# The retrieval layer of a decoder: three of four token tiles take gathered table rows, the fourth keeps the dense products

## The chip, the cores and the metric

The kernel runs on one core of one Trainium2 chip. The metric is the device time of one execution in microseconds. The whole decoder of twelve layers is one program; the change concerns the last layer alone.

## The reference

The layer is a memory of 4096 experts, each one row of a down table and one row of an up table, found by product keys, beside a small gated MLP. For each of 4096 tokens (B 4, T 1024, D 256):

```python
q = (x @ w_queries.T).reshape(b, t, 2, 4, 32)               # 2 sides, 4 heads
sim = einsum('btphn,hkpn->pbthk', q, keys)                  # 128 keys a side and head
sx, ix = top_k(sim[0], 8); sy, iy = top_k(sim[1], 8)
all_scores = (sx[..., :, None] + sy[..., None, :])          # 64 pairs a head
all_idx = ix[..., :, None] * 128 + iy[..., None, :]
scores, pos = top_k(all_scores, 8)
indices = take_along_axis(all_idx, pos)                     # above 4095: the last row is read
ew = silu(einsum('btd,bthkd->bthk', x, down_embed[indices])) * softmax(scores)
experts = einsum('bthk,bthkd->btd', ew, up_embed[indices])
mlp = silu(x @ w_gate.T) * (x @ w_up.T) @ w_down.T          # inner width 512
x = layernorm(x + mlp + experts)
```

A token has 4 heads x 8 picks = 32 picks.

## The kernel before

The residual stays in SBUF, transposed: `chip.xt` is [128, 2, 4096], features on the partitions in two chunks. The layer works on 32 tiles of 128 tokens. It gathers nothing. For each tile TensorE multiplies the tokens with all 4096 rows of the down table ("dots", 8 chunks of 8 matmuls, L3811), ScalarE takes silu of each chunk into `r_active` [128 rows, 32 blocks, 128 tokens], and VectorE multiplies this by a dense matrix of weights ("mix", L3981), nonzero where a token picked the row. TensorE then multiplies the result with all rows of the up table ("out", 8 chunks of 8 matmuls, L3851), adding to the MLP's result in PSUM.

The dense weights are made from one-hots. VectorE finds the keys (MAX8 and FIND_INDEX8, "keys", L3993 and L3991) and the best pairs ("pairs", L4010 and L4008). POOL decodes the position of a pair into the two key numbers ("decode", L3914 to L3943) and compares the second number with 0..127, one lane at a time (`r_second_hot`, L3950, 32 instructions a tile). VectorE makes the one-hot of the first number times the softmax weight (`r_first_hot`, L4034 and L4035). For each lane two small matmuls (L3824) put their product into PSUM: four batches of 16 matmuls a tile.

The order is written out by hand. `retrieval_slots` makes one list of steps for all engines: in slot s, tile s has its weights made and multiplied, tile s+1 its dots, tile s-1 its out product, tile s+2 its keys and pairs, tile s+3 its query projection ("project") and similarities ("sims"). A slot has 8 places, each with one chunk of dots and one of out. "gate" and "hide" are the MLP, "add" adds the residual into `norm_sum`, and "mean", "var", "spread" are the layer norm of a group of four finished tiles. Every engine walks the same list and does its part of each step; semaphores order them. The products of "project", "sims", "gate", "mean", "var" and "spread" go through a ring of two PSUM banks, each used in turn; dots, weights and outputs have two banks each. SyncE issues seven loads at the start, down table third, up table last.

`step(...)` (L51) opens a block with its own semaphores; `load`, `Chip` and the other layers are not touched. The line number of a semaphore wait at the end of a block is L56 or L64.

Of the kernel before, what the change touches and what calls it, by code (L numbers as in the profile page):

```python
# [5 lines left out]
F32 = mybir.dt.float32  # L6
# [7 lines left out]
P = 128  # L14
# [3678 lines left out]
LANES = SLOT // 2  # L3693
CHUNKS = 8
BATCHES = 4


def retrieval_slots():

    order = []  # L3700
    for s in range(-3, TOKEN_TILES + 2):
        closes = (s - 5) // PER_HALF if s >= 5 and s % PER_HALF == 1 else None
        places = [[] for _ in range(CHUNKS)]
        places[0] += [("add", s - 2, 0), ("exp", s + 1, 0), ("lanes", s, 1), ("decode", s + 1, 0)]
        places[1] += [("gate", s, 0), ("weights", s + 1, 0)]
        places[3] += [("hide", s, 0)]
        places[4] += [("project", s + 3, 0), ("turn", s + 1, 0), ("lanes", s + 1, 0)]
        places[6] += [("sims", s + 3, 0)]
        for n in range(RHEADS * SIDES):
            places[1 + n // 3].append(("keys", s + 2, n))  # L3710
        for n in range(RHEADS):
            places[5 + n // 2].append(("pairs", s + 2, n))
        places[7].append(("shift", s + 2, 0))
        for j in range(CHUNKS):
            here = [("mix", s, j // 2)] if j % 2 == 0 else []
            here += [("out", s - 1, j), ("dots", s + 1, j)] + places[j]
            order += [step_ for step_ in here if 0 <= step_[1] < TOKEN_TILES]
            if closes is not None:
                order += [(kind, closes, 0) for kind, at in (("mean", 1), ("var", 3), ("spread", 6)) if at == j]
    return order  # L3720


def retrieval_ffn(chip):
# [3 lines left out]
    order = retrieval_slots()  # L3727
    ring = {}
    for kind, t, n in order:
        for use in {"gate": ("gate", "up"), "sims": ("sims_0", "sims_1"), "project": ("project",), "mean": ("mean",), "var": ("var",), "spread": ("spread",)}.get(kind, ()):  # L3730
            ring[(use, t)] = len(ring)
    with ExitStack() as ctx:
# [4 lines left out]
        active = sb("r_active", [P, 2, BLOCKS, P])  # L3737
        second_hot, first_hot = sb("r_second_hot", [P, 2, LANES, KEYS]), sb("r_first_hot", [P, 2, LANES, 2 * BLOCKS])
# [17 lines left out]
        with step(nc, "search_loaded down_loaded mlp_loaded up_loaded ring_ready bank_read_0 bank_read_1 dots_ready dots_active weights_ready mixed hot_first hot_second "  # L3756
# [5 lines left out]
            def read_of(use, t):  # L3762
                r = ring[(use, t)]
                return bank_read[r % 2], r // 2 + 1
# [483 lines left out]
```

## Time and profile before

| | before |
|---|---|
| median of 3 runs | 10450.3 us (10445.38 to 10500.5) |
| profiled execution: its time | 10466.0 us |
| profiled execution: span | 10464.2 us |
| TensorE busy | 8774.6 us (84%) |
| VectorE busy | 5572.0 us (53%) |
| ScalarE busy | 4189.2 us (40%) |
| POOL busy | 2222.1 us (21%) |
| TensorE's mean granted clock | 0.892 of full |

PE is the matmul side of TensorE and PEld its weight loads; DVE is VectorE, ACT ScalarE, POOL GpSimd, SP SyncE. Names of tiles are printed without digits, L12 is line 12 of the kernel. The shares are means over the whole program; the layer that is changed fills the last 1500 us of it, and its rows are taken from there.

### The profile page before, as it was taken

The numbers are of one execution on the slowest core, as the hardware profiler recorded it, in microseconds if no ns is written. First come the engines' busy times: TensorE is split into PE (matmuls) and PEld (weight loads), VectorE is DVE, ScalarE is ACT, GpSimd is POOL, SyncE is SP. The second block draws the span as 40 slices with busy tenths as digits, with TensorE's granted clock in tenths as the row PEclk, the third lists the DMA queues.
The fourth block names the chain that finished last, engine by engine and source line by source line (L and its number), as shares of the span: only waits on it lengthen the run. The fifth ranks groups of instructions, "written<-read, shape, count | busy, mean of one in ns | idle before, by whom it ended". The sixth has DMA issues, their size and how long they took to land. (4 is left out here: it accounts for less than half of the span.)

```text
span 10464.2 us, 134852 instructions
## 1 busy us (share of the span) xinstructions
PE 8774.6 (84%) x51394; PEld 5200.4 (50%) x51506; DVE 5572.0 (53%) x9096; ACT 4189.2 (40%) x6715; POOL 2222.1 (21%) x2590
## 2 busy tenths in 40 slices
PE   4888583985898979999996988889886999999999
PEld 1222242652333346646643544444343444799998
DVE  6777441014776736526634887765544666343343
ACT  3666230111555546415622676652221444222221
POOL 1010112011111001101100443330000110566665
PEclk8888675985999989999997998989886999999999
DMA  3222142111222100000000000000001322100000
GB/s 67 41 41 41 36 66 78 65 57 39 41 41 41 24 22 1 4 13 7 1 4 14 1 1 1 1 3 8 6 1 29 58 45 44 44 1 1 1 1 17
DMA packets 161954, 263.21 MB, mean 25 GB/s; under 512 B 38699, under 2 KB 78485, under 8 KB 159543
## 3 DMA queue, kind: packets, MB, share of 16 engines
q1 hardware_dynamic: 155175, 240.91, 11.4%
q0 software_dynamic: 6144, 13.64, 0.4%
q8 instruction: 421, 6.90, 0.3%
q14 instruction: 214, 1.75, 0.1%
HBM read 165.30 MB, written 75.53 MB: 23 GB/s over the span
## 5 line engine op out<-in xcount | busy, mean ns | idle before, releaser
L819 ACT ACTIVATE probs<-scores 128x1024 f32<-128x1024 f32 (+4 forms) x960 | 868.4, 937 | 873.6 <-PE scores L696 618.4
L908 DVE TENSOR_REDUCE row_max<-ring 128x1 f32<-128x512 f32 (+3 forms) x1792 | 1025.4, 628 | 238.5 <-PE ring L670 213.5
L696 PE MATMUL scores<-query_stack,key_stack 99*128 99x512 bf16 (+3 forms) x2816 | 846.2, 391 | 164.4 <-DVE levels L930 77.8
L716 PE MATMUL outputs<-probs,head_values 128*32 128x512 f32 (+3 forms) x5632 | 778.5, 627 | 101.3 <-ACT probs L816 98.6
L3950 POOL TENSOR_SCALAR r_second_hot<-constants,r_picks_t 128x128 f32<-128x128 f32 x1024 | 662.2, 664 | 431.2 <-DVE r_picks_t L4027 431.2
L816 ACT ACTIVATE probs<-levels,quant 128x1024 f32<-128x1024 uint8 x512 | 612.7, 1233 | 330.3 <-DVE levels L930 327.0
L930 DVE TENSOR_SCALAR levels<-scores 128x1024 uint8<-128x1024 f32 x512 | 607.7, 1220 | 181.4 <-PE scores L696 149.3
L670 PE MATMUL ring<-key_stack,query_stack 96*128 96x512 bf16 (+3 forms) x1792 | 607.9, 382 | 62.5 <-DMA key_stack<-normed_parts 39.9
L696 PEld LDWEIGHTS scores<-query_stack,key_stack 99*128 99x128 bf16 x2816 | 256.6, 103 | 684.6 <-DVE levels L930 278.6
L3676 DVE TENSOR_TENSOR_SCAN ssm_pre<-ssm_pre,added 128x1024 f32<-128x1024 f32 x256 | 571.0, 2271 | 33.2 <-ACT ssm_pre L3634 33.2
L3891 ACT ACTIVATE r_active<-r_psum_dots 128x512 f32<-128x512 f32 x256 | 152.7, 597 | 999.4 <-PE r_psum_dots L3811 995.3
L3981 DVE TENSOR_TENSOR r_active<-r_psum_weights,r_active 128x1024 f32<-128x1024 f32 x128 | 156.8, 1225 | 713.5 <-PE r_psum_weights L3824 713.5
L3611 PE MATMUL state_sums<-term,constants 128*128 128x512 f32 x1024 | 493.4, 605 | 43.9 <-POOL term L3642 34.3
L3851 PE MATMUL r_psum_y<-r_active,r_up_rows 128*128 128x128 f32 x4096 | 511.0, 279 | 0.0
L3811 PE MATMUL r_psum_dots<-residual,r_down_rows 128*128 128x128 f32 x4096 | 502.5, 276 | 3.0 <-DMA r_down_rows<-in_L_ffn_down 2.5
L3029 POOL TENSOR_TENSOR norm_squares<-qk,rope 128x256 f32<-128x256 f32 x256 | 181.3, 743 | 1517.4 <-DVE qk L2953 1517.4
L3851 PEld LDWEIGHTS r_psum_y<-r_active,r_up_rows 128*128 128x128 f32 x4096 | 479.1, 192 | 18.9 <-issue 10.5
L3811 PEld LDWEIGHTS r_psum_dots<-residual,r_down_rows 128*128 128x128 f32 x4096 | 481.4, 193 | 5.2 <-DMA r_down_rows<-in_L_ffn_down 3.3
L670 PEld LDWEIGHTS ring<-key_stack,query_stack 96*128 96x128 bf16 x1792 | 171.0, 103 | 497.3 <-DVE row_max L908 298.4
L2760 PE MATMUL window_products<-wide_w,shifted 128*128 128x512 f32 x768 | 366.8, 629 | 53.8 <-DVE shifted L2930 45.2
L3648 POOL TENSOR_TENSOR added_rows<-ssm_du_rows,ssm_state_in_rows 128x384 f32<-128x384 f32 x256 | 208.3, 832 | 927.0 <-SPq L56 906.5
L3630 ACT ACTIVATE added_rows<-ssm_du_rows,ssm_state_in_rows 128x128 f32<-128x128 f32 x1280 | 398.1, 386 | 4.3 <-PEq L64 4.3
(657 smaller groups left out, 16553.3 us busy)
## 6 DMA issues: line engine op xcount, KB each, us to landing
joined_heads<-heads_out SPq DMA_DIRECT2D x512, 32.0 KB, 2.0
expert_w<-in_L_ffn_w SPq DMA_DIRECT2D x16, 1024.0 KB, 11.5
quant_parts<-parts SPq DMA_DIRECT2D x48, 256.0 KB, 5.2
query_stack<-quant_parts SPq DMA_DIRECT2D x48, 256.0 KB, 8.6
key_stack<-quant_parts SPq DMA_DIRECT2D x48, 256.0 KB, 8.4
query_stack<-cross_parts SPq DMA_DIRECT2D x48, 256.0 KB, 8.2
normed_parts<-parts SPq DMA_DIRECT2D x48, 256.0 KB, 4.8
query_stack<-normed_parts SPq DMA_DIRECT2D x48, 256.0 KB, 8.6
```

Of the source, the lines that this page charges most:

```text
L670: last = nc.tensor.matmul(out[:, 0:cols], lhs, k_stack[0:max_row, h, j * GROUP:j * GROUP + cols], start=True, stop=not edge)
L696: last = nc.tensor.matmul(out[:, off:GROUP], keys, q_stack[0:rows, h, half * GROUP + off:(half + 1) * GROUP], start=True, stop=not edge)
L716: last = nc.tensor.matmul(o_ps[SLOT * i:SLOT * (i + 1), half % out_banks, off:GROUP], vals, probs[0:k_rows, n % 2, i // 2, i % 2, off:GROU ...
L816: nc.scalar.activation(dst, levels[:, e % 2, :, :], ACT.Exp, bias=quant[:, 4:5], scale=scale).then_inc(probs_ready, 1)
L819: nc.scalar.activation(dst, s_ps[0:k_rows, 2 * (e % 2):2 * (e % 2) + 2, off:GROUP], ACT.Exp, scale=scale).then_inc(probs_ready, 1)
L908: nc.vector.reduce_max(row_max[:, i, qt, at:at + 1], src[:, 0:cols], AX.X).then_inc(ring_read, 1)
L930: ts(levels[:, e % 2, :, :], s_ps[:, 2 * (e % 2):2 * (e % 2) + 2, :], 0.0, QMAX, ALU.max, ALU.min).then_inc(scores_read, 1)
L3611: last = nc.tensor.matmul(sum_ps[:, half(j)], chip.c(C_ID), term[:, i % 2, half(j)], start=(n == 0), stop=(n == STATES - 1))
L3676: nc.vector.tensor_tensor_scan(state[:, i % 2, :], decay[:, i % 2, :], added[:, i % 2, :], 0.0, ALU.mult, ALU.add).then_inc(state_ready, 1)
L3811: last = nc.tensor.matmul(s_ps[:, k % 2, i * P:(i + 1) * P], down[:, c, row * P:(row + 1) * P], x(t, c), start=(c == 0), stop=(c == FC - 1))
L3851: last = nc.tensor.matmul(y_ps[:, t % 2, c * P:(c + 1) * P], up[:, row, c * P:(c + 1) * P], active[:, t % 2, row, :], start=False, stop=(r ...
L3950: last = ts(second_hot[:, n, q, :], chip.c(C_IOTA), picks_t[:, t % 2, 1, lane:lane + 1], None, ALU.is_equal)
```

## The change

Of each group of four tiles, the first three are now *fetched* and the fourth is *dense*.

For a fetched tile POOL issues 32 indirect DMAs (768 in all), one a pick: each brings for all 128 tokens their row of a new input `L3_ffn_tables` (down and up row side by side, 512 floats, 2 KB; padded to 16384 rows so that every index is valid) into one slot of the ring `r_got` of 16 slots. VectorE takes the dot product of the down half with the token's own features (`rows`, transposed back by TensorE and copied by ScalarE) with a tensor_tensor_reduce. After the eight dots of a head ScalarE takes silu ("live"), VectorE multiplies by the softmax share ("weigh"), ScalarE makes for each pick a diagonal matrix (identity times the 128 weights), and TensorE multiplies the up half of the slot with it, adding in PSUM ("mix", two matmuls a pick). POOL waits before every fourth gather until the four picks that used the slots are summed.

The dense tile goes the old way, with single instead of double buffers (`r_active`, the dots bank), batches of 8 lanes, and the second one-hot made by one VectorE instruction for 8 lanes. POOL's decoding moves to VectorE ("places", "codes", "picked"), shorter by a few instructions. POOL does nothing but gathers.

The new list `retrieval_events` runs in beats of eight rows. Fetched tile i has the beats 4i to 4i+3 (one head each); a group is 12 beats, all are 96. A beat has 8 places, one dot in each; the mixing of the head before stands in places 1 to 4. A tile's search is spread over five beats, three beats ahead of its gathers; the dense tile's dots take beats 1 to 8 of its group, its weights beats 8 to 13, its out product beats 13 to 20. The layer norm of a group now covers the dense tile of the group before and its own three fetched tiles, so there are 9 closings instead of 8. The load of the down table moves behind the three of the MLP.

The diff, cut to its core:

```diff
+GOT_ROWS = 16
+RELEASE = 4
+CYCLE = FETCHED * RHEADS
+def retrieval_events():
...
+    for g in range(GROUPS):
+        for r in range(PER_HALF):
+            t = PER_HALF * g + r
+            s = CYCLE * g + FETCHED * (r - 2)
+            put(s - 2, 5, "project", t)
+            put(s - 2, 7, "queries", t)
+            put(s - 1, 3, "sims", t)
+            put(s - 1, 5, "sims_copy", t)
+            for n in range(RHEADS * SIDES):
+                put(s + n // 4, 2 * (n % 4) + 1, "keys", t, n)
+            for n in range(RHEADS):
+                put(s + 2, 2 * n, "pairs", t, n)
+            put(s + 2, 7, "shift", t)
+            put(s + 3, 0, "places", t)
+            put(s + 3, 2, "exp", t)
+            put(s + 3, 3, "codes", t)
+            put(s + 3, 6, "picked", t)
+            put(s + 4, 3, "weights", t)
+        for r in range(FETCHED):
+            i = FETCHED * g + r
+            first = RHEADS * i
+            put(first - 3, 5, "gate", i, r)
+            put(first - 3, 6, "gated", i, r)
+            put(first - 2, 0, "multiplied", i, r)
+            put(first - 1, 5, "hide", i, r)
+            put(first - 2, 5, "rows", i)
+            put(first - 2, 7, "rows_copy", i)
+            put(first + RHEADS + 1, 2, "add", i, r)
         for j in range(CHUNKS):
+            put(CYCLE * g + 1 + j, 6, "dots", g, j)
+            put(CYCLE * g + 1 + j, 7, "silu", g, j)
+            put(CYCLE * (g + 1) + 1 + j, 5, "out", g, j)
+        put(CYCLE * g + 7, 4, "turn", g)
+        for n in range(BATCHES):
+            put(CYCLE * g + 8 + n, 7, "lanes", g, n)
+            put(CYCLE * g + 9 + n, 5, "weave", g, n)
+            put(CYCLE * g + 10 + n, 3, "blend", g, n)
...
+    for i in range(FETCHED_TILES):
+        for h in range(RHEADS):
+            k = RHEADS * i + h
+            for n in range(TOP):
+                plan.setdefault((k, n), []).insert(0, ("dot", k, n))
+            plan.setdefault((k + 1, 0), []).append(("live", k))
+            plan.setdefault((k + 1, 1), []).insert(0, ("weigh", k))
+            for n in range(TOP):
+                put(k + 1, 1 + n // 2, "mix", k, n)
...
+            @block.gpsimd
+            def _(pool):
+                for i in range(FETCHED_TILES):
+                    pool.wait_ge(decoded, searched[fetched_tile(i)] + 1)
+                    for n in range(PICKS):
+                        k = PICKS * i + n
+                        if k >= GOT_ROWS and n % RELEASE == 0:
+                            pool.wait_ge(summed, k - GOT_ROWS + RELEASE)
+                        nc.gpsimd.indirect_dma_start(out=got[:, k % GOT_ROWS, :], out_offset=None, in_=io["L3_ffn_tables"],
+                                                     in_offset=bass.IndirectOffsetOnAxis(ap=index[:, i % FETCHED, n:n + 1], axis=0)).then_inc(arrived[k % GOT_ROWS], 16)
...
+                    elif kind == "mix":                       # TensorE
+                        k, n = which
+                        i = k // RHEADS
+                        pe.wait_ge(diagonal_ready, TOP * k + n + 1)
+                        for c in range(FC):
+                            last = nc.tensor.matmul(y_of(i, 0)[:, c * P:(c + 1) * P], got[:, (TOP * k + n) % GOT_ROWS, DIM + c * P:DIM + (c + 1) * P], diagonal[:, n, :],
...
+                    elif kind == "live":                      # ScalarE
+                        k = which[0]
+                        act.wait_ge(dot_ready, TOP * (k + 1))
+                        nc.scalar.activation(act_w[:, k % 2, :], dot[:, k % 2, :], ACT.Silu).then_inc(live_ready, 1)
+                    elif kind == "mix":
+                        k, n = which
+                        if n == 0:
+                            act.wait_ge(weighted, k + 1)
+                        if k:
+                            act.wait_ge(summed, TOP * (k - 1) + n + 1)
+                        nc.scalar.activation(diagonal[:, n, :], chip.c(C_ID), ACT.Copy, scale=act_w[:, k % 2, n:n + 1]).then_inc(diagonal_ready, 1)
...
+                    if kind == "dot":                         # VectorE
+                        k, n = which
+                        at, i = TOP * k + n, k // RHEADS
...
+                        if n == 0 and k >= 2:
+                            dve.wait_ge(diagonal_ready, TOP * (k - 1))
+                        dve.wait_ge(arrived[at % GOT_ROWS], 16 * (at // GOT_ROWS + 1))
...
+                        nc.vector.tensor_tensor_reduce(scratch[:, at % 2, :], got[:, at % GOT_ROWS, 0:DIM], rows[:, i % 2, :], 1.0, 0.0, ALU.mult, ALU.add,
+                                                       dot[:, k % 2, n:n + 1]).then_inc(dot_ready, 1)
+                    elif kind == "weigh":
+                        k = which[0]
+                        dve.wait_ge(live_ready, k + 1)
```

## Rows read from the trace of the kernel before

**Rows 1.** Windows: a stretch of the retrieval step, busy us of each engine.

```profile
core 0: us, PE busy (x) PEld busy (x) DVE busy (x) ACT busy (x) POOL busy (x), PEclk, DMA share, GB/s
9000.00:10400.00 1400.00, 1399.15 (x13698) 1339.78 (x13697) 544.98 (x1594) 322.77 (x488) 931.21 (x1506) 1.00 0.01 1
```

**Rows 2.** Chain of waits: start us, us, engine, line; counts include the weight loads.

```profile
9014.91 1.72 PE r_psum_ring L3801 x4
...
9026.82 1.79 PE r_psum_dots L3811 x16
9028.60 3.57 PE r_psum_ring L3833 x32
9032.18 1.93 PE r_psum_weights L3824 x32
```

**Rows 3.** Chain of waits: first and last pieces of the step.

```profile
8948.16 0.42 SPq L3772
...
10441.68 1.97 PE r_psum_ring L3859 x4
...
10445.77 1.93 PE r_psum_ring L3866 x16
...
10448.35 1.45 PE r_psum_ring L3872 x8
...
10449.82 0.69 DVE residual L4050
```

**Rows 4.** Instructions of one line: durations in ns, min/median/max.

```profile
L3950 POOL TENSOR_SCALAR r_second_hot<-constants,r_picks_t x1024: 590/596/1679, 8974.5 to 10405.1; 128x128 f32<-128x128 f32 x171
...
L4035 DVE TENSOR_TENSOR r_first_hot<-r_first_hot,r_picks_t x64: 1224/1274/2209, 8975.7 to 10403.4; 128x1024 f32<-128x1024 f32 x64
```

**Rows 5.** Timeline of POOL, expert layer: start us, us, instruction, idle before.

```profile
2303.02 0.94 POOL L2563 DMA_INDIRECT got<-produced,place_now  x1 [0.30 <-issue]
...
2315.51 0.94 POOL L2563 DMA_INDIRECT got<-produced,place_now  x1 [0.30 <-issue]
```

**Rows 6.** DMA, 2296 to 2330: GB/s in 40 slices; packets, MB, share.

```profile
GB/s 0 0 53 101 120 87 101 111 96 101 111 145 53 130 116 63 140 140 29 130 149 58 87 183 48 116 0 0 0 0 0 0 0 0 0 0 0 0 10 0
...
q0 software_dynamic: 768, 2.10, 23.3%
```

**Rows 7.** Timeline of VectorE: the first tile's search.

```profile
8959.39 0.28 DVE L3991 FIND_INDEX8 r_best_at<-r_best,norm_squares 128x8 uint32<-128x128 f32 x1
...
8959.85 0.28 DVE L3991 FIND_INDEX8 r_best_at<-r_best,norm_squares 128x8 uint32<-128x128 f32 x1
...
8962.57 0.41 DVE L4003 TENSOR_TENSOR r_sums<-r_best 128x256 f32<-128x256 f32 x1
...
8964.33 0.17 DVE L4016 TENSOR_TENSOR r_weight<-r_score 128x32 f32<-128x32 f32 x1
```

**Rows 8.** Timeline of VectorE in the expert layer.

```profile
2320.75 0.48 DVE L2576 SCALAR_TENSOR_TENSOR mixed<-got,gate_now,mixed 128x256 f32<-128x256 f32 x1
2321.15 0.35 DVE L2575 TENSOR_SCALAR mixed<-got,gate_now 128x256 f32<-128x256 f32 x1
```

**Rows 9.** The page's costliest groups: busy us, mean ns of one, idle before.

```profile
L3676 DVE TENSOR_TENSOR_SCAN ssm_pre<-ssm_pre,added 128x1024 f32<-128x1024 f32 x256 | 571.0, 2271 | 33.2 <-ACT ssm_pre L3634 33.2
```

**Rows 10.** Timeline of ScalarE: scaled copies in another layer, a table load here.

```profile
5902.90 1.55 ACT L3630 ACTIVATE added_rows<-ssm_du_rows,ssm_state_in_rows 128x128 f32<-128x128 f32 x5
5904.35 1.14 ACT L3634 ACTIVATE ssm_pre<-ssm_dt,a_log 128x1024 f32<-128x1024 f32 x1
...
8963.79 1.28 ACT L3891 ACT_TABLE_LOAD   x1
```

**Rows 11.** Windows of three other layers, columns as in rows 1.

```profile
200.00:400.00 200.00, 160.65 (x827) 50.61 (x820) 155.31 (x166) 132.38 (x119) 20.51 (x14) 0.89 0.18 34
...
5800.00:6000.00 200.00, 186.04 (x765) 102.57 (x764) 172.41 (x98) 144.11 (x332) 113.03 (x85) 0.99 0.00 1
8400.00:8600.00 200.00, 181.85 (x1363) 93.10 (x1363) 116.87 (x255) 92.88 (x124) 25.89 (x18) 0.92 0.34 55
```

**Rows 12.** Instructions of one line: the gathers of the expert layer.

```profile
L2563 POOL DMA_INDIRECT got<-produced,place_now x64: 942/946/1011, 2296.7 to 2419.9; - x64
```

More of the change, by code:

```diff
@@ L3692 @@
 TURN = P // SLOT
-LANES = SLOT // 2
+LANES = 8
 CHUNKS = 8
[L3695 to L3713, printed above, removed]
-        for j in range(CHUNKS):
[L3715 to L3720, printed above, removed]
@@ L3726, in retrieval_ffn @@
     rc = RINNER // P
-    order = retrieval_slots()
+    events = retrieval_events()
+    uses = {"gate": ("gate", "up"), "sims": ("sims_0", "sims_1"), "project": ("project",), "rows": ("rows",), "mean": ("mean",), "var": ("var",), "spread": ("spread",)}
     ring = {}
-    for kind, t, n in order:
-        for use in {"gate": ("gate", "up"), "sims": ("sims_0", "sims_1"), "project": ("project",), "mean": ("mean",), "var": ("var",), "spread": ("spread",)}.get(kind, ()):
-            ring[(use, t)] = len(ring)
+    for kind, *which in events:
+        for use in uses.get(kind, ()):
+            ring[(use, *which)] = len(ring)
+    searched = {t: n for n, t in enumerate(which[0] for kind, *which in events if kind == "picked")}
+    adds = {tuple(which): n + 1 for n, which in enumerate(which for kind, *which in events if kind == "add")}
     with ExitStack() as ctx:
@@ L3810, in _ @@
+                        for i in range(PER_CHUNK):
+                            row = PER_CHUNK * j + i
                             for c in range(FC):
-                                last = nc.tensor.matmul(s_ps[:, k % 2, i * P:(i + 1) * P], down[:, c, row * P:(row + 1) * P], x(t, c), start=(c == 0), stop=(c == FC - 1))
+                                last = nc.tensor.matmul(s_ps[:, i * P:(i + 1) * P], down[:, c, row * P:(row + 1) * P], x(PER_HALF * g + FETCHED, c), start=(c == 0), stop=(c == FC - 1))
@@ L3821, in _ @@
                             for r in range(2):
[L3822 removed]
+                                half = slice(P // 2 * r, P // 2 * (r + 1))
                                 out = w_ps[:, r, :].rearrange("p (s q i) -> p q s i", s=2, i=BLOCKS)[:, q, :, :]
[L3824 removed]
+                                last = nc.tensor.matmul(out, second_hot[half, q, :], first_hot[half, q, :], start=True, stop=True)
@@ L3854, in _ @@
                             last.then_inc(y_ready, 1)
                     elif kind == "mean":
-                        out = free_bank("mean", t)
-                        pe.wait_ge(added, PER_HALF * (t + 1))
+                        cols = closing(which[0])[0]
+                        out = free_bank("mean", *which)
+                        for n, r in ([(which[0] - 1, FETCHED)] if which[0] else []) + ([(FETCHED * which[0] + FETCHED - 1, FETCHED - 1)] if which[0] < GROUPS else []):
+                            pe.wait_ge(added, adds[(n, r)])
@@ L3864, in _ @@
-                        for p in range(PER_HALF):
+                        out = free_bank("var", *which)
+                        pe.wait_ge(c_squared, FC * (which[0] + 1))
+                        for p in closing(which[0])[2]:
                             for c in range(FC):
```

418 lines of the change are left out of this document (245 added, 173 removed).

## The prediction

> **What bounds the kernel now.** I read the page first, to see that only the last layer, the retrieval step, is touched, and then the windows of that step. In the 1400 us from 9000 to 10400 TensorE is busy in 1399.15 and its granted clock is 1.00; VectorE is busy in 545, ScalarE in 323, POOL in 931, the DMA engines in 1% [rows 1]. The step is bound by TensorE alone. The chain of waits says the same: it runs from one matmul group to the next, with no other engine between [rows 2]. A tile costs two dense products over all 4096 rows (16 chunks of 8 matmuls, 1.79 us a chunk), four groups of 16 small matmuls that make the weights (1.93 us each), gate and up (3.57), down (8 matmuls, as a chunk, 1.79), sims (1.72), the projection (four matmuls of the same 0.223 us, 0.9) and its share of a normalisation, 1.3. These are 45 to 46 us, and 32 tiles of it fill the step. The step begins with SyncE's first load at 8948.2 and its last VectorE piece ends at 10450.5 [rows 3]: 1502 us. Before and behind it nothing changes.
>
> **The unit of the new order.** It runs in beats: one head of one fetched tile, eight picks, is a beat, 3 tiles x 4 heads = 12 beats make a group of four tiles, 8 groups make 96 beats. So the new step is lead-in + 96 x T + tail, and the whole question is T. Four resources each have a floor for T.
>
> **TensorE.** Removed, in three tiles of four: both dense products (28.6 us) and the weights (7.7). Added there: 32 picks x 2 matmuls (64 x 0.223 = 14.3 us) and two transposes (0.45). Per group: mixing 42.9, dense dots and out of one tile 28.6, its weights 7.7, gate and up 14.3, down 7.2, projection 3.8, sims 6.9, transposes 1.3, closing matmuls 5.4 (1.97 + 1.93 + 1.45 [rows 3]). The sum is 118 us, or 9.84 us a beat, where four tiles cost 181 before. All this is at full clock.
>
> **POOL.** Its decoding and its 1024 one-hots (596 ns each [rows 4]) go; it only issues gathers, 768 of them. The layer with the experts has the same instruction: eleven of them start from 2303.02 to 2315.51, one in 1.25 us, 0.95 busy and 0.30 between [rows 5]. A row there is 1 KB per partition, here 2 KB, but the number of rows is 128 in both, so I keep 1.25: 10.0 us a beat, 960 in all. If the busy part went by bytes it would be 2 x 0.95 + 0.30 = 2.2 us (17.6 a beat); no row speaks for that, since the index list is what the instruction works through, and it stands as the far bound, with the price of rival (C).
>
> **DMA engines.** 16 to 17 of those gathers (2.10 MB) took 23.3% of 16 engines in 34 us [rows 6], 0.48 us for each. A new one moves twice the bytes: 0.48 us if the price goes by rows, 0.96 by bytes, so 3.8 to 7.7 us a beat. They are not the bound. The last gather is issued by 2316.5 and traffic ends in the slice that ends at 2318.1 (slices of 0.85 us [rows 6]), so a row lands some 1.6 us after its issue, 2.6 after its start.
>
> **VectorE.** Neighbouring instructions overlap, so I count start to start. Kept per tile: eight key searches at 0.46, pairs and shift from 8962.57 to 8964.50, three short ones of 0.2: 6.3 us [rows 7]. Taken over from POOL per tile: about eight short ones at 0.2 and three of 128x512 at 0.7 (0.69 [rows 3]): 3.7 us. Added: 96 dots of 128x256 with a sum. No row has this instruction. The plain two-input form of that shape lasts 0.41, or 0.33 start to start by the overlap seen [rows 7]; the scalar form lasts 0.48 and its successor starts 0.40 behind it [rows 8]; the scan's 2.2 ns an element would make 0.57 [rows 9]. I take 0.40, as nearest in kind, bounds 0.33 and 0.57. Per group: search 25, decoding 15, dots 38 (32 to 55), one-hots 10.4 (1.2 + 0.7 + 0.7, four times), blends 4.8, the rest (multiply, add, centre, scale, weigh) 10. That is 103 us, 8.6 a beat (8.1 to 10.0). ScalarE adds 96 scaled copies of 128x128; five of these run from 5902.90 to 5904.35, 0.29 each [rows 10]: 28 a group. With silus, copies and ten table loads of 1.28 [rows 10] it is near 61, 5.1 a beat. It is no bound, but a table load in front of a copy delays TensorE by 1.3 us.
>
> **How they meet.** Three floors, 10.0, 9.84 and 8.6, lie almost on one another, and each beat's work differs. TensorE's beats go from 7 us (weights and mixing) to 13.6 (mixing, two chunks, gate and up, projection, mean), VectorE's from 5.7 to 12.3 (decoding beside one-hots). The largest of the three in each of the 12 beats, added up, is 134 us, T = 11.1; perfect smoothing gives 10.0. The coupling allows only a part of it. A beat's dots are followed by silu, weighing, scaled copies and matmuls one beat later. While VectorE waits for the silu, the next dots and searches are queued behind it; while TensorE waits for the scaled copies, its chunks and the gate are, and for these VectorE's multiply waits a beat later. POOL reissues four slots when their four rows are summed. A row is held for 2.6 us plus some 1.35 beats, of the two beats that 16 slots last; at T = 11 the slack is 4.6 us, less than the overrun of some beats put together, and POOL, itself at its floor, can't catch up. TensorE, which now waits, also loses clock. Stages in which several engines take turns show what is left of it: busy share times granted clock is 0.71, 0.92 and 0.84 [rows 11]. With 9.84 us of work a beat these give T = 13.9, 10.7 and 11.7. I take the middle one, T = 11.7.
>
> **Lead-in and tail.** The key searches begin near 8959, the first shift is done at 8964.5 [rows 7]; decoding adds 3.7, the next tile's searches between some 1.8, the first gather 2.6: beat 0 starts near 8972.5, 24 us after the step began. On SyncE's queue the load of the down table moves behind those of the MLP; its reader comes a beat later, and that hides it. Behind beat 95: mixing 3.6, dense out 8 x 1.79, add 0.4, and a closing of one tile, about 5 where four tiles take 8.8 [rows 3]: 24 us. Together 48.
>
> **Sum.** 48 + 96 x 11.7 = 1171, against 1502: 331 less. The profiled execution took 10466.0 with a span of 10464.2; the median of the three is 10450.3, 16 below. Median predicted: 10450 - 331 = 10120.
>
> **The rivals.** (A) Smooth: POOL's pace alone, T = 10.0 to 10.8. At 10.0 the step is 1008, the time 9956. For it: the other floors are lower. Against: the uneven beats and the small slack. (B) The coupling costs more: a ring of two beats that starves POOL whenever TensorE overruns, table loads in the path, a clock that falls with the waits. T = 13 to 14.6; at 13.9 the step is 1382 and the time 10330. The share of 0.71 speaks for it, the two others against. (C) Slower, by one mechanism: a gather's issue is stretched while VectorE works from SBUF. Break-even is T = 15.15, a gather every 1.89 us. VectorE's instructions with two SBUF inputs (dots, comparisons, one-hots) would fill about 57 of 120 us; were the 0.95 us stretched to double by that, a gather would take 2.2, T = 17.6, step 1738, time 10686. For it: beside POOL's work, VectorE's 128x1024 multiply goes from 1224 to a median of 1274 and at most 2209 ns, and a POOL one-hot from 590 to at most 1679 [rows 4]. Against: the medians are 4% and 1% over the minima, not double, and 64 gathers lie within 942 to 1011 ns [rows 12], though hardly one of them ran beside such an instruction.
>
> The Trainium skill (SBUF — State Buffer, "Who interferes with whom") says that a two-input VectorE instruction takes only the read side of what it shares with GpSimd, that writing descriptors needs the write side, and that copies and tensor-scalars in a two-port mode are what block a GpSimd DMA. By that rule only the short decoding copies would hold gathers up, an estimated 6 us of a group, and T would grow by at most 0.5; no row here shows it.
>
> **How the numbers follow.** Forecast, T = 10.8 to 13.0 (10033 to 10244): 0.53. (A): 0.12. (B): 0.20. T near break-even, within 0.5%: 0.05. (C) and what else is slower: 0.10. A change within 0.5%, 52 us, is about what a measurement of this kernel can't tell from none. Faster is 0.85, same 0.05, slower 0.10. The range takes in the case of POOL's pace almost to its floor (T = 10.2, 9975) and (B) up to T = 13.9 (10330); VectorE's upper bound for the dots (10.0 a beat) lies inside.
>
> **What would show it.** Right: gathers start 1.25 us apart at the least; TensorE is busy in 85 to 90% of the step at a clock of 0.90 to 0.97; waits for dots are put down to gathers or ring slots; the step lasts 1130 to 1300 us. Wrong: a DMA_INDIRECT clearly over 1 us (C); a clock near 0.8 and long waits of TensorE for scaled copies (B); dots over 0.6 us, which makes VectorE the bound.

## The result and the profile after

The changed kernel takes 10667.4 us (median of 4 runs, 10659.2 to 10676.5) against 10464.9 for the kernel before, measured beside it: ratio 1.0186, 95% interval 1.0167 to 1.0206. The forecast was 10120, with a range of 9975 to 10330 and 0.85 for faster. It is slower, outside the range. By the formula of the prediction, T = (time - 8996) / 96, a beat lasts 17.4 us instead of 11.7. This T is the time in another unit, and so are those of the runs below (the expectations use values lower by 0.2). In the trace, from the first dot (8972.99) to the mixes of the last beat (10610.10), a beat lasts 17.05 us.

The windows of the retrieval step (its bounds, then busy time of each engine, granted clock, share of the DMA engines, GB/s) answer to [rows 1]:

```profile
9000.00:10600.00 1600.00, 1128.71 (x7832) 1044.68 (x7832) 732.08 (x3334) 457.93 (x1170) 733.55 (x744) 0.81 0.42 123
```

No engine is the bound now: TensorE is busy in 71% of the step and at a clock of 0.81, POOL in 46%, VectorE in 46%. The groups of that stretch (busy, mean ns | idle before them and what ended it) answer to [rows 4, 5, 10]:

```profile
L3856 POOL DMA_INDIRECT r_got<-in_L_ffn_tables,r_index x744 | 733.6, 986 | 866.6 <-PE r_psum_y L3913 598.7 <-issue 199.3 <-DVE r_index L4136 64.9
L3913 PE MATMUL r_psum_y<-r_diagonal,r_got 128*128 128x128 f32 x2980 | 550.8, 361 | 413.1 <-ACT r_diagonal L4011 351.4 <-issue 60.8
L4054 DVE CUSTOM_DVE_ANT_0 r_scratch<-r_got,r_rows 128x256 f32<-128x256 f32 x747 | 299.8, 418 | 230.6 <-issue 138.6 <-DMA r_got<-in_L_ffn_tables,r_index 89.2
L4011 ACT ACTIVATE r_diagonal<-constants,r_act 128x128 f32<-128x128 f32 x749 | 231.9, 388 | 85.7 <-DVE r_act L4060 47.5 <-issue 38.2
```

The prices are as forecast: a gather 986 ns and 0.30 behind it, a dot 418, a copy 388. What is new is the waiting: POOL waits 599 us for summed slots, TensorE 351 for scaled copies, and the copies in turn for the engines before them. The waits (total, times, longest) show one more, with a releaser called "remote", which says that the profile found no instruction of this core that ended the wait:

```profile
ACT r_active L4015 <- remote: 367.7, 42, 14.1
DVE r_act L4060 <- ACT r_act L4004: 235.3, 36, 9.8
```

L4015 is the silu of a chunk of the dense tile. It needs only TensorE's dots. The timeline of one beat shows when it starts (a matmul stands in it as two records, so x16 is eight matmuls, and this is so in [rows 2] too, where the count holds no weight loads):

```profile
9634.93 1.95 PE L3926 MATMUL r_psum_dots<-residual,r_down_rows 128*128 128x128 f32 x16
9636.33 0.95 POOL L3856 DMA_INDIRECT r_got<-in_L_ffn_tables,r_index  x1 [0.30 <-issue]
9637.58 0.96 POOL L3856 DMA_INDIRECT r_got<-in_L_ffn_tables,r_index  x1 [0.31 <-issue]
9640.12 0.60 ACT L4015 ACTIVATE r_active<-r_psum_dots 128x512 f32<-128x512 f32 x1 [11.63 <-remote]
9640.61 0.20 ACT L4004 ACTIVATE r_act<-r_dot 128x8 f32<-128x8 f32 x1
9641.05 2.45 ACT L4011 ACTIVATE r_diagonal<-constants,r_act 128x128 f32<-128x128 f32 x8 [0.23 <-DVE r_act L4060]
9641.50 3.79 PE L3913 MATMUL r_psum_y<-r_diagonal,r_got 128*128 128x128 f32 x16 [4.62 <-ACT r_diagonal L4011]
9645.56 0.95 POOL L3856 DMA_INDIRECT r_got<-in_L_ffn_tables,r_index  x1 [7.02 <-PE r_psum_y L3913]
```

The dots end at 9636.88, and the silu starts 3.24 us later, 1.58 us after POOL's last gather of the burst ended (9638.54). Behind it, in ScalarE's order, stand the fetched dots' silu (L4004), the weighing, the copies, the mixes, the release of the slots and the next burst. The mixes follow an idle TensorE, and the first eight of their 16 matmuls take 3.79 us where eight dots took 1.95: the granted clock is 0.50 in this stretch, the lower of its two levels. That is one closed loop a beat. Over the step, where ScalarE stood waiting for such dots, the silu came 3.2 us late in the median (48 cases, at most 5.1) with gathers in flight, and 0.04 us late in all 6 without. Signals from ScalarE to VectorE and back, and from ScalarE to TensorE, arrive within 0.1 us of the instruction's end in either case. The semaphores' own records agree on TensorE: of some 1100 signals of TensorE's matmuls in the step 227 come more than 0.5 us after the matmul's end.

The trace of the kernel before holds the same thing, in the layer whose gathers I read for their price [rows 5, 12], but I read POOL's rows alone. TensorE, ScalarE and POOL there, the kernel before:

```profile
2338.44 3.14 PE L152 MATMUL norm_psum<-constants,norm_squares 128*128 128x1 f32 x16 [0.36 <-ACT norm_squares L171]
2341.91 0.26 ACT L174 ACTIVATE norm_root<-norm_psum,epsilons 128x4 f32<-128x4 f32 x1 [2.22 <-PE norm_psum L152]
2348.01 0.95 POOL L2563 DMA_INDIRECT got<-produced,place_now  x1 [0.30 <-issue]
2351.90 0.26 ACT L174 ACTIVATE norm_root<-norm_psum,epsilons 128x4 f32<-128x4 f32 x1 [9.73 <-remote]
```

The second root needs the matmuls that end at 2341.58; it starts 10.3 us later, 2.9 us after the last gather.

### The profile page after: what moved, and what is told of

It reads as the page before. It is cut to its first block and busy times, and to the rows that moved or that the text cites. A ratio compares the mean times of both kernels' runs of the same rounds, so it can differ in the third digit from the quotient of the medians.

```text
span 10658.2 us, 125232 instructions
## 1 busy us (share of the span) xinstructions
PE 8477.9 (80%) x45414; PEld 4874.6 (46%) x45414; DVE 5768.9 (54%) x10917; ACT 4326.3 (41%) x7413; POOL 2009.7 (19%) x1790
## 5 line engine op out<-in xcount | busy, mean ns | idle before, releaser
L3856 POOL DMA_INDIRECT r_got<-in_L_ffn_tables,r_index x768 | 757.2, 986 | 1084.2 <-PE r_psum_y L3913 605.4
L3913 PE MATMUL r_psum_y<-r_diagonal,r_got 128*128 128x128 f32 x3072 | 565.3, 361 | 431.2 <-ACT r_diagonal L4011 369.6
L3913 PEld LDWEIGHTS r_psum_y<-r_diagonal,r_got 128*128 128x128 f32 x3072 | 533.0, 269 | 480.3 <-ACT r_diagonal L4011 397.1
L4054 DVE CUSTOM_DVE_ANT_0 r_scratch<-r_got,r_rows 128x256 f32<-128x256 f32 x768 | 308.3, 418 | 244.9 <-issue 143.8
L3634 ACT ACTIVATE ssm_pre<-ssm_dt,a_log 128x1024 f32<-128x1024 f32 x256 | 292.4, 1142 | 127.2 <-DVE ssm_pre L3676 127.1
L3602 PEld LDWEIGHTS added<-constants,added_rows 128*128 128x128 f32 x2048 | 245.2, 145 | 165.6 <-issue 137.2
L631 PE MATMUL ring<-norm_sum,split_w 128*128 128x512 f32 x384 | 201.1, 653 | 123.2 <-DVE norm_sum L254 99.5
```

The source lines that it names most:

```text
L3856: nc.gpsimd.indirect_dma_start(out=got[:, k % GOT_ROWS, :], out_offset=None, in_=io["L3_ffn_tables"], in_offset=bass.IndirectOffsetOnAxis( ...
L3913: last = nc.tensor.matmul(y_of(i, 0)[:, c * P:(c + 1) * P], got[:, (TOP * k + n) % GOT_ROWS, DIM + c * P:DIM + (c + 1) * P], diagonal[:, n ...
```

## The experiments

Three theories. **S**: while gathers are in flight, TensorE's completions are seen late. **L**: the order itself closes a loop once a beat and costs this with any signals. **R**: the ring of 16 slots starves POOL. All times are medians. The kernel before took 10465 to 10483 us in these sets, and the changed kernel 10667 to 10732 in the four that have it, so differences of times across sets are good to some tens of us; each ratio is against its own set. Runs e1 to e4 shared one chip, e5 to e9 a second, e10 to e13 a third.

### One wait moved

```diff
-            put(CYCLE * g + 1 + j, 7, "silu", g, j)
+            put(CYCLE * g + 2 + j, 5, "silu", g, j)
```

> The silu of a chunk of the dense tile moves from the last place of its beat to place 5 of the next, behind the eight scaled copies, so that it no longer stands ahead of the silu of the fetched dots on ScalarE. Theory L (a closed loop of TensorE, ScalarE and VectorE once a beat is what the step waits for): in 8 of 12 beats the loop gets shorter by the 3 to 4 us for which ScalarE waits for the dense dots now, T from 17.2 to 14 to 15, time 10350 to 10450. Theory S (TensorE's completions are seen late while gathers are in flight, whatever the order): the wait moves to the next instruction that depends on TensorE, T 16.5 to 17.2, time 10600 to 10667. Theory R (POOL refills a ring that is too short): no change, within 50 us of 10667.

10537.5 us, ratio 1.0051 (1.0035 to 1.0067), T = 16.1. 130 us come from moving this wait alone (1.35% by the ratios). The loop is real, but no theory's number fits: L promised more (217 to 317 us), S at most 67.

### The same bytes without gathers

Run e2 replaces each gather, e3 leaves out all but 16, e4 gathers 64 bytes a row (edits in short form here and in the next two sections):

```diff
-  pool: indirect_dma_start(got[:, slot, :], tables, index[:, tile, n:n + 1])
+  e2, SyncE: dma_start(got[:, slot, :], tables[k % 128 * P:(k % 128 + 1) * P, :])
+  e3, pool: only for k < GOT_ROWS
+  e4, pool: indirect_dma_start(got[:, slot, 0:16], narrow, index[:, tile, n:n + 1])
```

> Part of the computation is changed: the 768 gathers of POOL become 768 plain loads of SyncE with the same bytes into the same slots, of 128 neighbouring rows of the table in place of the picked ones; all waits stay. Theory S: TensorE's completions are seen at once (within 0.1 us), T 12 to 13.5, time 10200 to 10340. Theory L alone: the loop stays, the pace of the issue goes, T 16 to 17, time 10550 to 10650. If late completions come from any DMA traffic, they stay late here too and the time stays above 10600. [...]

> Part of the computation is left out: only the first 16 rows are gathered, all later dots and mixes read these, and POOL and the DMA engines are idle from then on. What stays is the coupling of TensorE, ScalarE and VectorE. Theory S: close to my forecast's coupled beat, T 11.5 to 13, time 10150 to 10300, and TensorE's completions on time. Theory L: T 14 to 16, 10390 to 10580, since the loop has no gather in it. Theory R: T 10.5 to 12, below 10200, since no slot is ever waited for.

> Part of the computation is changed: each of the 768 gathers brings 64 bytes of a row instead of 2 KB, into the front of its slot; the rest of the slot holds rows loaded once. 128 rows a gather stay, the bytes fall to a thirty-second. If late completions come with bytes in flight, T falls as in the run with SyncE's loads, 12 to 13.5, time 10200 to 10340. If they come with the issue or the number of rows of a POOL gather, they stay 3 to 8 us late and the time stays above 10600. A gather's instruction stays at 0.95 us in both.

e2: 10223.1 us, ratio 0.9747 (0.9723 to 0.9770). e3: 10217.9, ratio 0.9748 (0.9722 to 0.9775). e4: 10707.6, ratio 1.0215 (1.0189 to 1.0242). So the order with completions on time runs at T = 12.8, in the upper part of my range (by the trace a beat of 12.3 us in e2 and in e5 below); all traffic of the rows costs no more than the noise hides (e2 and e3 are 5 us apart); and a thirty-second of the bytes costs as much as all of them. In e2 and in e3 the silu follows the dots within 0.04 us in all 64 chunks. R falls: e3 never waits for a slot and gains nothing on e2. The windows of e2, over 1100 us:

```profile
9000.00:10100.00 1100.00, 926.64 (x7509) 859.48 (x7510) 692.03 (x3240) 439.95 (x1119) 0.00 (x0) 0.94 0.52 169
```

TensorE is busy in 84% of it at a clock of 0.94, and the DMA engines move more a second than they do in the changed kernel.

### Which property of the gathers

```diff
+  e5, pool: dma_start(got[:, slot, :], tables[k % 128 * P:(k % 128 + 1) * P, :])
+  e10, pool: indirect_dma_start(got[:, slot, :], tables, order[:, 0:1])   # row p for partition p
+  e9: even picks gathered by pool, odd picks loaded by SyncE as in e2
```

> Part of the computation is changed: POOL issues 768 plain loads of 128 neighbouring rows each, of the same bytes into the same slots, instead of indirect gathers. Against the run in which SyncE issued these very loads (10223 us) only the issuing engine differs. Theory S1 (any transfer whose descriptors POOL writes makes TensorE's completions late): time 10550 to 10700, silu of the dense dots 2 to 4 us behind their end. Theory S2 (only the indirect form does): completions on time, 10200 to 10300.

> Part of the computation is changed: all 768 gathers stay indirect and stay on POOL, but take a fixed index, row p for partition p, so that they read 128 neighbouring rows as the plain loads did (10221 us). If the scattered addresses make TensorE's completions late: time 10200 to 10300. If it is the indirect form itself: completions 2 to 4 us late as before, 10620 to 10690.

> Part of the computation is changed: POOL gathers the even picks only (384 gathers), SyncE loads 128 neighbouring rows for each odd pick. Theory S by the share of time with gathers in flight: half of the 445 us that the gathers cost against SyncE's loads, T near 15, time 10400 to 10480. If one gather in flight at the wrong moment is enough, the time stays above 10560; if lateness needs gathers back to back, it falls to 10220 to 10320.

e5: 10221.2 us, ratio 0.9764 (0.9737 to 0.9791). e10: 10707.3, ratio 1.0205 (1.0177 to 1.0233). e9: 10296.8, ratio 0.9836 (0.9816 to 0.9856). Plain loads through POOL's own queue do no harm, gathers of neighbouring rows do all of it: it is the indirect form, not the queue, the bytes or the addresses. One thing goes with the form and isn't separated here: POOL's pace, a plain load starting 0.53 us behind the last and a gather 1.25. In e5 POOL loads, and the silu follows the dots (9516.95) at once; timeline of e5:

```profile
9513.67 2.12 POOL L3856 DMA_DIRECT2D r_got<-in_L_ffn_tables  x4 [1.38 <-PE r_psum_y L3912]
9515.00 1.95 PE L3925 MATMUL r_psum_dots<-residual,r_down_rows 128*128 128x128 f32 x16
9516.98 0.60 ACT L4014 ACTIVATE r_active<-r_psum_dots 128x512 f32<-128x512 f32 x1 [4.76 <-PE r_psum_dots L3925]
```

Half of the gathers, in bursts of four, cost 74 us against e2, all of them 444. The time lies in the last of my three ranges (lateness needs gathers back to back), and the records agree: of the 64 signals of the dense dots 6 are more than 0.5 us late in e9, 47 in the changed kernel. Half as many gathers also ask half as much of POOL, so the 74 us don't tell the two apart.

### Gathers beside a dense TensorE

The kernel before, with gathers (e12) or plain loads (e13) from POOL that nobody reads:

```diff
                         last.then_inc(hot_second, 1)
+                        if n == 1: ... for m in range(8):
+  e12:                      indirect_dma_start(spare[:, m, :], narrow, order_at[:, 0:1])
+  e13:                      two dma_start of 32 bytes a row into spare[:, m, :]
```

> The kernel before, and POOL also issues eight indirect gathers of 64 bytes a row behind its last one-hot of each tile, 256 in all, into a tile that nobody reads. TensorE is the bound here and has two banks of everything. If only its completions are late (by 2 to 4 us, against 3.6 us of slack in the two banks of dots): silu starts late, TensorE stays dense, time within 40 us of before. If the matmuls themselves are held up: 10 of 46 us of a tile are under gathers, at a half to a third longer 100 to 150 us, 10580 to 10630. POOL's added 10 us a tile fit into its 15 idle ones.

> Control for the run before it: in place of eight gathers POOL issues sixteen plain loads (0.53 us each, 8.5 us a tile) into the same tile. Completions on time, time within 30 us of the kernel before. If it is as slow as the run with gathers, POOL's added time was the cause there and not the gathers.

e12: 10595.5 us, ratio 1.0101 (1.0079 to 1.0124): 256 gathers cost 118 us. e13: 10494.0, ratio 1.0009 (0.9991 to 1.0026): the loads cost nothing that can be told. The time is that of my second reading, but the matmuls are not held up in the way I had meant, as longer ones. Timeline of e12, TensorE and ScalarE in a burst from 9536.88 to 9546.92:

```profile
9537.61 1.95 PE L3813 MATMUL r_psum_dots<-residual,r_down_rows 128*128 128x128 f32 x16
9539.39 1.95 PE L3853 MATMUL r_psum_y<-r_active,r_up_rows 128*128 128x128 f32 x16
9541.18 1.95 PE L3813 MATMUL r_psum_dots<-residual,r_down_rows 128*128 128x128 f32 x16
9542.97 1.95 PE L3835 MATMUL r_psum_ring<-residual,r_gate_w 128*128 128x128 f32 x16
9544.75 1.95 PE L3835 MATMUL r_psum_ring<-residual,r_up_w 128*128 128x128 f32 x16
9547.57 0.21 PE L3826 MATMUL r_psum_weights<-r_first_hot,r_second_hot 64*128 64x64 f32 x1 [0.28 <-issue]
9548.27 1.66 PE L3826 MATMUL r_psum_weights<-r_first_hot,r_second_hot 64*128 64x64 f32 x25 [0.48 <-issue]
9548.36 0.60 ACT L3899 ACTIVATE norm_sum<-r_psum_ring 128x512 f32<-128x512 f32 x1 [3.76 <-remote]
9549.86 3.28 PE L3853 MATMUL r_psum_y<-r_active,r_up_rows 128*128 128x128 f32 x16
```

Chunks start 1.79 us apart under the gathers, as in [rows 2]: their matmuls are not longer. The gate's silu (L3899) comes 3.4 us after the gate's product, 1.44 after the last gather. TensorE itself pauses with nothing to wait for ("issue"), and the next product takes 3.28 us instead of 1.95, with a granted clock of 0.59 from 9549.9 to 9553.0. In 1400 us TensorE is busy 1360 instead of 1399 and its clock is 0.96 instead of 1.00: by an estimate from these two 39 and 56 us, which is most of the 118. Why TensorE pauses isn't shown. Late signals are there too: 83 of 617 come more than 0.5 us late, in e13 and in the kernel before none.

### Order against lateness

e7 moves the copies of queries and rows, the gate's silu and the root one beat on, ahead of the scaled copies; e8 is e2 with the silu moved as in e1; e11 is e7 with two gathers in flight:

```diff
-            put(s - 2, 7, "queries", t)          # rows_copy, root likewise
+            put(s - 1, 0.5, "queries", t)
-            put(first - 3, 6, "gated", i, r)
+            put(first - 2, 0.5, "gated", i, r)
+  e11:                  pool.wait_ge(arrived[(k - 2) % GOT_ROWS], 16 * ((k - 2) // GOT_ROWS + 1))
```

> The real gathers stay. Beside the silu of the dense dots (which gave 130 us) the other ScalarE instructions that read TensorE's newest results at the end of a beat (the copy of the queries, the copy of the token rows, the MLP's silu, the root) move to the next beat, behind the silu of the fetched dots, and VectorE's multiply of the MLP from place 0 to place 2. Theory S with the loop: each of them now waits in the shadow of the weighing, T from 15.9 to 15.0 to 15.6, time 10440 to 10510. If late completions just move the wait on, within 30 us of the 10537 of the run with the silu alone.

> Part of the computation is changed as in the run with SyncE's loads (10223 us, T = 12.6), and the silu of the dense dots moves behind the scaled copies as in the reordered run. Theory L (the closed loop costs time by itself, also with completions on time): T 11.3 to 12.1, time 10100 to 10180. If the order matters only because completions are late, within 25 us of 10223.

> The order of the 10478 us version, and POOL waits before each gather until the row of the last but one has landed: gathers start 1.7 to 2.0 us apart instead of 1.25, so eight take 14 to 16 us. If completions get through in the gaps of 0.8 us: T 14.5 to 15.2, time 10400 to 10460. If a completion needs a gap of 1 to 1.8 us behind a gather, as in the trace, the bursts only get longer: T 17 to 19, time 10620 to 10800.

e7: 10478.4 us, ratio 1.0007 (0.9992 to 1.0022), T = 15.4. e8: 10110.2, ratio 0.9658 (0.9639 to 0.9677), T = 11.6. e11: 10566.7, ratio 1.0071 (1.0047 to 1.0094). The silu's place costs 113 us with completions on time and 130 with late ones (0.9 and 1.35% by the ratios), so L is right about a real but small part, and most of what e1 gained would have come without lateness too. Spacing the gathers (e11) is worse than e7 by 88 us: they start 2.0 us apart in the median, so that eight take 16 us, and by the trace a beat lasts 16.1. TensorE's signals do get through in the gaps (60 of 1094 are more than 0.5 us late, in e7 378), so this is a time that POOL's pace sets and lateness doesn't. The expectation had the signals on time and the pace too small.

### Late completions out of the loop

In e14 ScalarE reads everything of TensorE's at place 5.5 of the next beat, behind the scaled copies, TensorE makes it behind its mixes, and VectorE's first wait for the weaving comes a beat later. All gathers are real. e15 is that order with e2's loads. The diff is cut to its core.

```diff
-            put(s - 2, 5, "project", t)
-            put(s - 2, 7, "queries", t)
-            put(s - 1, 3, "sims", t)
+            put(s - 4, 6, "project", t)
+            put(s - 3, 5.5, "queries", t)
+            put(s - 2, 6, "sims", t)
-            put(first - 3, 6, "gated", i, r)
+            put(first - 2, 5.5, "gated", i, r)
-            put(CYCLE * g + 1 + j, 7, "silu", g, j)
+            put(CYCLE * g + 2 + j, 5.5, "silu", g, j)
-            put(CYCLE * g + 8 + n, 7, "lanes", g, n)
+            put(CYCLE * g + 9 + n, 2.9, "lanes", g, n)
...
```

> All real gathers, all of the computation. Every result of TensorE is now read by ScalarE or VectorE in the beat after the one that makes it, behind the scaled copies, so that nothing that TensorE signals late stands ahead of the fetched dots' silu, the weighing, the copies and the mixes. If what is left of the gathers' cost is that a late completion stands in that chain: one burst of gathers (10 us) and one wait for completions (1 to 1.8 us) make a beat, T 11.5 to 13.5, time 10100 to 10300, faster than before. If a late completion costs the same wherever it is read, T stays at 15 to 15.5, time 10440 to 10500.

> Part of the computation is changed: the order of the run before this one with SyncE's plain loads in place of the gathers. It gives that order's time with completions on time: T 10.6 to 11.5, time 10030 to 10120. The distance to the run with real gathers is what the gathers cost in this order, against 368 us in the order that moves the silu, the queries and the gate.

e14: 10232.1 us, ratio 0.9779 (0.9766 to 0.9793), T = 12.9. e15: 10090.6, ratio 0.9643 (0.9622 to 0.9664), T = 11.4. The number of e14 is the one that I had promised for late completions that stand outside the loop. Its trace says something else: in the whole retrieval step no record of a TensorE signal is more than 0.5 us late, gathers or not. Nor is one in the expert layer, which no experiment touches. The groups of that layer from 2290 to 2430 us, its root on ScalarE, which waits for TensorE; the kernel before, then e14:

```profile
L174 ACT ACTIVATE norm_root<-norm_psum,epsilons 128x4 f32<-128x4 f32 x6 | 1.6, 263 | 35.7 <-remote 33.5 <-PE norm_psum L152 2.2
```

```profile
L174 ACT ACTIVATE norm_root<-norm_psum,epsilons 128x4 f32<-128x4 f32 x8 | 2.1, 264 | 6.1 <-PE norm_psum L152 6.1
```

This wait marks the chip. It is 32 to 36 us in the traces of before, after and e1 to e13, and 6.1 and 4.5 us in e14 and e15, which ran together on another chip. So this chip, or its state in that set, has no late completions, and the two don't test S. They do show what real gathers cost without lateness in this order: 142 us, 1.4%.

### The changed kernel and the one-hop order on one chip

e16 is the changed kernel, e17 is e14, unaltered. e18 and e19 are the changed kernel on two further chips.

> The changed kernel once more, unaltered. In the traces of all runs but the last two, the norm of the expert layer (no part of the change) has ScalarE wait 33 to 36 us beside the gathers there; in the last two (one hop, real and with SyncE's loads) it waits 4.5 to 6 us, and no completion in the retrieval step is late either. If lateness belongs to the chip or its state: where the expert layer's wait is 33 us, 10640 to 10690 with late completions; where it is 5 us, completions on time and 10220 to 10330, as with plain loads. If it belonged to the kernel: 10640 to 10690 whatever that wait is.

> The one-hop order once more, on the chip of the run before this one. If its 10232 us came from an undisturbed chip alone: on a chip with late completions it is slower than 10232, but faster than 10478 (the version that moves less) if taking late completions out of the loop helps, 10280 to 10400; near 10478 if it doesn't help. On an undisturbed chip: 10220 to 10245 again, and what the order is worth there is its distance to the unaltered changed kernel, 0 to 100 us.

> The changed kernel a third time, unaltered, for its time where the expert layer's wait is about 5 us. There: 10220 to 10330, since the completions are on time, as with plain loads (10223). If this time depends on the kernel and not on the chip's state: 10650 to 10700. Where the wait is 33 us again, 10650 to 10700 by both, and the run tells nothing new.

> The changed kernel a fourth time, for the same question and with the same two answers: 10220 to 10330 where the untouched expert layer waits about 5 us, if the loss belongs to late completions; 10650 to 10720 where it waits 33 us.

The mark is 36.0 and 34.9 us in e16 and e17, 40.3 and 36.6 in e18 and e19: late completions in all four. e16: 10691.5 us, ratio 1.0207 (1.0182 to 1.0232). e17: 10423.4, ratio 0.9949 (0.9931 to 0.9967), T = 14.9. e18: 10722.8, ratio 1.0235 (1.0217 to 1.0252). e19: 10731.8, ratio 1.0249 (1.0220 to 1.0279). So the one-hop order is worth 268 us under late completions (2.6% by the ratios) and ends half a per cent below the kernel before; one more order, e7, had only drawn level. Not all of the 268 is lateness avoided: with plain loads the same order is worth 1.0% (e2 against e15). It doesn't reach 10232: the same kernel costs 191 us more where completions are late. The gathers cost 4.6% of before's time in the changed order (1.0207 against e2's 0.9747), 3.1% in the one-hop order (0.9949 against 0.9643), and 1.4% in it on the chip without late completions.

What keeps e17 behind e14 is only in part known. ScalarE and VectorE hardly wait for late signals any more (8 times, 19 us; in the changed kernel 72 times, some 230 us). But about 320 of the 768 signals by which the mixes release the slots are late in e17, and TensorE pauses where the profile finds nothing to wait for. The largest sums of such pauses in e17, from 9000 to 10100:

```profile
PE r_psum_y L3913 <- issue: 78.3, 87, 5.2
PE r_psum_ring L3895 <- issue: 31.1, 43, 6.2
```

In all these are 130 us in 150 pauses; e14 has none in the same stretch, and e5 none.

Windows of the three, over the same 1100 us: e16, e17, and e14:

```profile
9000.00:10100.00 1100.00, 768.71 (x5386) 707.96 (x5387) 507.20 (x2334) 317.20 (x806) 500.52 (x510) 0.82 0.42 122
```

```profile
9000.00:10100.00 1100.00, 854.11 (x6249) 779.19 (x6249) 605.81 (x2742) 371.00 (x939) 591.01 (x597) 0.86 0.49 145
```

```profile
9000.00:10100.00 1100.00, 921.43 (x7383) 859.78 (x7384) 706.81 (x3172) 427.39 (x1094) 703.24 (x694) 0.91 0.57 166
```

Every engine does more from one row to the next and the clock rises: nothing got cheaper, TensorE stood idle less.

## Why the prediction was wrong

- **What bounds the kernel now, lead-in, prices.** Right, but for one term. The first dot starts at 8972.99 (forecast 8972.5). A gather a 1.25 us, a dot 0.42 start to start (0.40), a copy 0.30. The tail was sized too short: from the mixes of beat 95 to VectorE's last piece 34 us, not 24.
- **DMA engines.** By bytes, not rows: 0.42 of 1600 us for 744 gathers is 0.90 us each, my upper end (0.96). A row lands 3.6 us after its start in the median, not 2.6. Run e3, where none has to land, puts the price of both near zero.
- **Rival (C).** Refuted: the mean gather is 986 ns, the longest 1791, where doubling of all was needed. The Trainium skill (SBUF — State Buffer, "Who interferes with whom") was cited for this; the trace agrees in so far as, beside the comparisons and dots of VectorE, half of the gathers last 943 to 949 ns.
- **"How they meet".** This is the step that failed, in two unequal parts. It took one term, the share of TensorE's busy time times its clock, as 0.84 from stages without gathers [rows 11]; measured it is 0.79 in e2 and 0.57 in the changed kernel (0.71 times 0.81), and 9.84 us over these gives 12.4 and 17.2, close to the beats of 12.3 and 17.05 in the traces. So TensorE's 9.84 us of work were right and its share was wrong.
  - The small part, with completions on time: e2, e3 and e5 are about 100 us above the forecast, inside my own range of 10.8 to 13.0. Some 60 us of it are the beat (12.3, not 11.7), 10 the tail, and 18 to 33 the kernel before, slower in these sets than the 10450 that I started from. I had listed what is queued behind each wait, but not that ScalarE's silu of the dense chunk stands ahead of the silu of the fetched dots and so ties TensorE's last product of a beat to its first of the next; taken away, T is 11.6 (e8).
  - The large part, 444 us (after against e2; 4.4%), comes with the indirect gathers and not with bytes or addresses (e4, e5, e10). The prediction has no term for it. The three stages from which I took the coupling hold no gather of POOL, and in the layer that has them I read the price of the instruction and not who waited beside it. What stands in its place is TensorE's completions, late while gathers are in flight: where ScalarE or VectorE stood waiting for them in the changed kernel, the lateness adds up to some 230 us. That this is on the path is shown by the order: the gathers' cost falls from 4.4% through 3.9% (e1 against e8) to 3.1% (e17 against e15), by the ratios, as fewer of these waits stand in the loop. How the rest divides isn't shown. TensorE's pauses and lower clock have a part in it, and so may POOL's pace; that gathers cost 1.4% in e14 without any lateness speaks for the latter.
- **Rival (B)** named the symptoms (clock near 0.8, waits for scaled copies) but bounded them at 14.6, from a stage without gathers. Its clock goes with the waits: the mixes behind TensorE's wait of 4.62 us ran at 0.50.
- **Break-even** at T = 15.15: e7 with 15.4 comes out even (1.0007). As T is reckoned from the time by the sum itself, this tests nothing; what tests the sum is the first dot, the tail and the beats above.

Not settled: what a chip must be like to have late completions (seven sets of runs had them, on at least six chips, one set on a seventh had none), and so the changed kernel's time on the one without; it was tried three times more and fell on chips with them each time. That would say how much of the 444 us vanishes there, and so how much is lateness and how much POOL's pace. Not settled either: whether TensorE's results are late in PSUM or only their signal. The Trainium skill (Perfetto Trace Analysis, Tensor Engine Instruction) says that the profile's end of a matmul is an estimate and that PSUM's acknowledgement pushes the semaphore afterwards. By that either could be; the rows show only that the distance grows from 0.04 to 3.2 us. Nor is it shown what in an indirect transfer does it, why a plain load from the same queue doesn't, or whether TensorE's pauses and its late signals have one cause.

## What to carry to other kernels

When a change adds an instruction that another stage already has, read there what all the other engines do beside it, not only its duration: a wait put down to "remote", or a consumer that starts microseconds after its producer's end, is a price too. Where POOL gathers beside a pipelined TensorE, let nothing that TensorE has just made stand ahead of the chain that frees the gathers' slots, but read it one beat later behind that chain; here that was worth 268 us on one chip, of which about 1.0 of 2.6% came without lateness too, and it took a third off what the gathers cost (4.6 to 3.1%). Before two sets of runs are compared, look in a stage that no kernel touches whether the chips behave alike. And sum a pipeline's coupling along each in-order queue, wait by wait, before taking a share from other stages.

## What the hardware showed

- On six of seven chips completions of TensorE are seen 3.2 us late (median of 48, up to 5.1) while indirect gathers of POOL run back to back, and in the three bursts shown they come 1.4 to 2.9 us after the last gather ended. It is the same with 64 bytes or 2 KB a row and with neighbouring or scattered rows (254 and 230 signals over 0.5 us late, 227 in the changed kernel); plain loads of POOL or SyncE at 169 to 170 GB/s leave them at 0.04 us. On the seventh chip gathers at 166 GB/s leave them at it too.
- It isn't proportional: half of the gathers cost 74 us where all cost 444, with 6 of 64 dense signals late instead of 47. Gathers 2.0 us apart instead of 1.25 leave 60 of 1094 signals late.
- A TensorE that is the bound loses too: 256 gathers, 118 us, with pauses put down to "issue" and a clock of 0.96 instead of 1.00.
- POOL's plain load of 128 rows of 2 KB takes 538 ns, an indirect one 986.
